# Rounds of outer products turned over, their bias moved into the relu, and every relu of the loop on ACT

## The reference

```python
x = e; xk = x; outs = []
for i in range(3):
    z = jnp.einsum('bfe,bge->bfge', x, xk).reshape(B_, F_ * F_, E_)   # products of fields f and g
    z = jnp.swapaxes(z, 1, 2)
    z = jnp.einsum('bcl,oc->bol', z, Ws[i]) + bs[i][None, :, None]    # sum over c, the 256 numbers e, for each pair l
    z = jnp.sum(jax.nn.relu(z), axis=-1)
    outs.append(z)                                                    # 16 numbers a sample
    xk = jnp.broadcast_to(z[:, :, None], (B_, F_, E_))
h = jnp.concatenate([outs..., dense_ctx], axis=1)                     # 48 + 16 features
h = jnp.maximum(h @ W_top1 + b_top1, 0.0)
h = jnp.maximum(h @ W_top2 + b_top2, 0.0)
y = h @ W_top3
```

## Time and profile before

| | |
|---|---|
| median of 3 runs | 565.79 us |
| the profiled execution | 566.43 us |
| its span (first to last instruction) | 564.6 us |
| PE busy / DVE / ACT / POOL | 536.8 / 524.9 / 404.4 / 452.8 us |
| granted clock of TensorE | 1.0 of full speed |
| a group in the steady part of the loop | 32.9 us |

### The profile page before, as it was taken

The page is one execution under the profiler, slowest core; times in us unless marked ns, Lnnn a source line. Parts: engine busy times, 40 slices in busy tenths (PEclk is TensorE's granted clock), DMA queues, the critical chain, the costliest instruction groups (busy, mean ns, idle before and its releaser), DMA issues.

```text
span 564.6 us, 19182 instructions
## 1 busy us (share of the span) xinstructions
PE 536.8 (95%) x8160; PEld 331.5 (59%) x8160; DVE 524.9 (93%) x234; ACT 404.4 (72%) x1217; POOL 452.8 (80%) x548
## 2 busy tenths in 40 slices
PE   2776899999999999999999999999999999999997
PEld 1433455666656566665656666565666656566566
DVE  5899899999999999999999999999999999999752
ACT  3575685877878687787868688786877778687743
POOL 6899999897988989798897979889897988988100
PEclk9999999999999999999999999999999999999999
DMA  3622323232232322223232222323232222322000
GB/s 91 172 73 70 91 67 92 63 72 81 67 80 65 96 58 75 79 66 81 64 96 58 69 85 67 79 65 96 58 76 76 64 82 68 91 63 63 17 2 2
DMA packets 27974, 40.67 MB, mean 72 GB/s; under 512 B 16880, under 2 KB 17264, under 8 KB 27888
## 3 DMA queue, kind: packets, MB, share of 16 engines
q0 software_dynamic: 12288, 33.57, 21.0%
q1 hardware_dynamic: 15600, 5.87, 4.7%
HBM read 38.77 MB, written 0.66 MB: 70 GB/s over the span
## 4 chain that ended last, share of the span: by engine, by line
PE 84%; POOL 7%; issue 4%; DVE 3%; DMA 1%; ACT 1%; POOLq 0%; DVEq 0%
PE sum_ps L701 39%; PE turn_ps L681 11%; PE outer_ps L776 9%; PE outer_ps L799 6%; PE sum_ps L716 4%; PE outer_ps L788 4%; POOL emb L291 4%; PE outer_ps L760 3%; DVE prods L237 2%; PE outer_ps L824 2%; POOL prods L304 1%; POOL prods L237 1%; PE outer_ps L808 1%; PE sum_ps L724 1%; PE sum_ps L710 1%
## 5 line engine op out<-in xcount | busy, mean ns | idle before, releaser
L237 DVE TENSOR_TENSOR prods<-turn_ps,emb_t 128x3360 f32<-128x3360 f32 (+2 forms) x126 | 452.7, 3608 | 11.9 <-ACT emb_t L518 10.1
L291 POOL DMA_INDIRECT emb<-tables,rows_sb x256 | 252.1, 985 | 44.1 <-issue 36.2
L701 PE MATMUL sum_ps<-prods,w_sb 128*32 128x272 f32 x4096 | 263.0, 398 | 1.1 <-POOL prods L237 1.0
L701 PEld LDWEIGHTS sum_ps<-prods,w_sb 128*32 128x32 f32 x4096 | 121.0, 110 | 96.0 <-issue 14.3
L545 ACT ACTIVATE relu<-sum_ps,bias_twice 128x120 f32<-128x120 f32 x256 | 91.6, 368 | 92.9 <-PE sum_ps L701 92.3
L304 POOL TENSOR_TENSOR prods<-emb_t 128x256 f32<-128x256 f32 x128 | 95.4, 746 | 32.1 <-ACT emb_t L518 30.0
L517 ACT COPY emb_t<-turn_ps 128x512 f32<-128x512 f32 (+1 forms) x126 | 75.7, 601 | 39.1 <-PE turn_ps L681 19.9
L681 PE MATMUL turn_ps<-ident_sb,emb 128*128 128x128 f32 x502 | 83.2, 288 | 9.2 <-issue 3.7
L237 POOL TENSOR_TENSOR prods<-emb_t 128x224 f32<-128x224 f32 (+1 forms) x128 | 83.9, 655 | 2.1
L556 ACT ACTIVATE relu_k<-outer_ps 128x2048 f32<-128x2048 f32 x44 | 83.8, 1904 | 2.2 <-PE outer_ps L776 2.2
L535 ACT ACTIVATE prods<-emb_t 128x512 f32<-128x512 f32 x128 | 83.7, 654 | 0.2
(11 more groups left out here) (99 smaller groups left out, 288.7 us busy)
## 6 DMA issues: line engine op xcount, KB each, us to landing
emb<-tables,rows_sb POOLq DMA_INDIRECT x256
z_wide<-z_spread SPq DMA_DIRECT2D x15, 256.0 KB
z_spread<-z_cat SPq DMA_DIRECT2D x60, 2.0 KB
w_sb<-w_top SPq DMA_DIRECT2D x1, 512.0 KB
z_spread<-z_wide SPq DMA_DIRECT2D x2, 256.0 KB
w_sb<-w_top SPq DMA_DIRECT2D x1, 256.0 KB
ids_sb<-ids_t SPq DMA_DIRECT2D x1, 129.0 KB, 2.2
z_cat<-dense_b SPq DMA_DIRECT2D x1, 128.0 KB
```

Source lines behind the costliest of these rows:

```text
L237: eng.tensor_tensor(out, every, shifted, ALU.mult).then_inc(done, 1)
L291: nc.gpsimd.indirect_dma_start(out=emb[:, k % EMB_RING, t * E:(t + 1) * E], out_offset=None, in_=tables, in_offset=bass.IndirectOffsetOnAx ...
L701: last = nc.tensor.matmul(sum_ps[s * 2 * F:(s + 1) * 2 * F, k % 2, 0:SUM_COLS], w_sb[:, c, odd, :], x[:, c, 2 * s + odd, :, :], start=c == ...
```

## The change

The two operands of a round's products trade places. `proj_b` becomes the stationary operand (its columns are picked with a step of two, since k is now innermost) and `z_wide` the moving one, 512 columns wide. So (f, o) come out on the partitions, 8 f x 16 o to a round, and (g, sample) along the columns. The output o is then a matter of the partition, and the bias is an operand `bias_k[:, k]` of the relu, one number per partition. The bias matmuls are gone, and so are their preparation on DVE, two loads in SP's queue, and the memset of the ones tile on POOL. A round is four fp32 matmuls of 512 columns in place of four bf16 ones of 512 and eight fp32 ones of 256.

All four relus of a group's rounds are on ACT; `relu_add` is gone. The fold of layer 2 therefore takes both rounds, as that of layer 1 does. After the fold, `reduce_fields` sums into a small tile `z_sum` and then transposes it into `z_cat`, two DVE instructions in place of one, with a wait between them. The columns of `z_cat` change places (dense features first). The wait for `z_wide` of layer 0 (`z_wide_in`) moves from the round into the last quarter of the same slot's `sum_pairs`.

```diff
@@ relu on ACT
-                nc.scalar.activation(relu_k[:, k, q, :, :, :].rearrange("p j h n -> p (j h n)"),
-                                     outer_ps[:].rearrange("p j n -> p (j n)"), ACT.Relu).then_inc(outer_relu, 1)
+                nc.scalar.activation(relu_k[:, k, q, :, :].rearrange("p j n -> p (j n)"), outer_ps[:].rearrange("p j n -> p (j n)"),
+                                     ACT.Relu, bias=bias_k[:, k:k + 1]).then_inc(outer_relu, 1)
@@ ACT's loop
-                if slot - 1 in ROUND_AT and (ROUND_AT[slot - 1][0], ROUND_AT[slot - 1][2]) != (1, 1):
+                if slot - 1 in ROUND_AT:
                     relu_round(*ROUND_AT[slot - 1])
@@ DVE
-            def relu_add(g):
...
-                nc.vector.scalar_tensor_tensor(out=second, in0=outer_ps[:].rearrange("p j n -> p (j n)"), scalar=0.0,
-                                               in1=first, op0=ALU.max, op1=ALU.add).then_inc(outer_relu, 1)
-            def reduce_fields(k, g):
+            def reduce_fields(k, g, src):
                 dve.wait_ge(fold_done[k], g + 1)
-                nc.vector.tensor_reduce(z_cat[:, g, (k + 1) * F:(k + 2) * F],
-                                        outer_ps[:, FOLD_BANK[k], 0:P].rearrange("p (f o) -> p o f", o=F),
-                                        AX.X, ALU.add).then_inc(z_ready[k], 1)
+                nc.vector.tensor_reduce(z_sum[:, k, :], src.rearrange("p (r a) -> p r a", r=R), AX.X, ALU.add).then_inc(z_summed[k], 1)
+                dve.wait_ge(z_summed[k], g + 1)
+                if k == 1:
+                    dve.wait_ge(z_ready[0], g + 1)
+                nc.vector.transpose(z_cat[:, g, Z_AT[k + 1]:Z_AT[k + 1] + R], z_sum[:, k, :]).then_inc(z_ready[k], 1)
@@ PE, sum_pairs
+                                if (c, odd, s) == (1, 1, 1) and (g := group_at(k, ROUNDS[0])) is not None:
+                                    pe.wait_ge(z_wide_in, 16 * (g + 1))
@@ PE, a round
-                b = bias_wide[:, k, :].rearrange("p (h n) -> p h n", h=1).broadcast_to([P, HALF_G, F * F])
-                for j in range(J):
-                    if q == 0 and j == 0:
-                        pe.wait_ge(proj_ready if k == 0 else z_ready[0], g + 1)
...
-                    if q == 0 and j == 3 and k == 0:
-                        pe.wait_ge(z_wide_in, 16 * (g + 1))
-                    if q == 0 and j == 3 and k == 1:
-                        pe.wait_ge(z_wide_ready[1], g + 1)
-                    nc.tensor.matmul(outer_ps[:, j, :], ones_sb[j * R:(j + 1) * R, :], b[j * R:(j + 1) * R, :, :],
-                                     start=True, stop=False)
-                products_of_round(k, g, q, [outer_ps[:, j, :] for j in range(J)])
+                for j in ((2, 3, 0, 1), (0, 1, 2, 3))[k]:
+                    if q == 0 and j == 2 and k == 0:
+                        pe.wait_ge(proj_ready, g + 1)
+                    if q == 0 and j == 0 and k == 1:
+                        pe.wait_ge(z_wide_ready[1], g + 1)
...
+                    last = outer_product(k, g, q, j, outer_ps[:, j, :])
+                last.then_inc(outer_done, 1)
+            def outer_product(k, g, q, j, out):
+                y = proj_b[j * R:(j + 1) * R, g % PT_RING, :].rearrange("p (n k) -> p k n", k=2)
+                return nc.tensor.matmul(out, y[:, k, q * HALF_F * F:(q + 1) * HALF_F * F],
+                                        z_wide[j * R:(j + 1) * R, k, :, :].rearrange("p q n -> p (q n)"), start=True, stop=True)
@@ PE, fold
-                first = k * HALF_G
-                for q in range(first, G4):
-                    for half in range(2):
-                        for j in range(J):
...
+                for q in range(TURNS):
+                    last = add_round(k, q, outer_ps[:, FOLD_BANK[k], 0:P], q == 0, q == TURNS - 1)
+            def add_round(k, q, out, first, final):
+                for n in range(G4):
+                    for j in range(J):
+                        last = nc.tensor.matmul(out[j * R:(j + 1) * R, :], fold_sb[:], relu_k[:, k, q, j, n * P:(n + 1) * P],
+                                                start=first and n == 0, stop=final and n == G4 - 1)
```

More of the change, by code:

```diff
@@ L340, in _ @@
                 half_shift(slot + 1)
+                if (g := group_at(slot, Z_BUILD)) is not None:
+                    z_spread(g)
                 gather(slot + 1 + LEAD, 1)
@@ L709, in turn_features @@
                 for half in range(2):
[L710 removed]
+                    last = nc.tensor.matmul(out[half * CAT:(half + 1) * CAT, :], z_cat[:, g, 0:CAT], ident_sb[:], start=True, stop=True)
                 last.then_inc(z_t_done, 1)
```

149 lines of the change are left out of this document (42 added, 107 removed).

## The result

The changed kernel takes 577.67 us, the median of four runs (576.91 to 581.25), against 565.76 us for the kernel before beside it. The ratio of the means is 1.0225, with a 95% interval of 1.0189 to 1.0261, a fifth run of 578.50 us included: slower by 2.2%, while the two medians are 2.1% apart. The forecast was 576.0 us with a range of 570 to 580. The profiled execution is the slowest of the four, 581.25 us with a span of 579.4; it is 14.8 us above the span of before, while the medians are 11.9 apart. Beyond the other traces of rounds turned over it has a late start, which is told further down.

The account below looks back on a forecast made before the run. PE was taken to bound the loop, with ACT holding stretch D. Twelve groups at +0.83 gave +9.9; start +0.4, last group +0.4, end -0.4: +10.3 on 566.43, 576.7, as a median 576.0 us, range 570 to 580.

Parts of the forecast that it names:

- the fold: Layer 2's fold on PE takes both rounds, 64 records instead of 32: +0.875 us a group, on PE's path.
- The round at 1.06 to 1.07: A round on PE drops its bias matmuls but loads its first weights bare: 1.06-1.07 us instead of 1.20, saving about 0.12.
- Two rounds of layer 2 save 0.24: On PE, layer 2's two shorter rounds were to take 0.24 us off each steady group.
- POOL's tie "as today": Layer 2's round waits for POOL's spreading of z at its first matmul, not its fourth: 0.01 us later at most.
- Stretch D, +0.22: From layer 1's first-round pair sum to its fold, held by ACT: 7.65 us plus 0.22 for bias in two relus.
- The relu on ACT at nothing: The 1.9 us relu that DVE gives up to ACT in slot 18 costs nothing; ACT's free time soaks it up.
- The moved wait, at something in the first group alone: Wait for z_wide's DMA, about half a microsecond earlier, in the pair sums: +0.8 us in the first group, where it bit once.
- The start, +0.4, bounds -0.5 to +1.0: First group: moved wait +0.8, fold +0.3, a vanished wait for DVE -0.6; taken as +0.4 us as a whole.
- The last group and the end, 0 together: Last group +0.4 us, with no fold behind its D; end section -0.4, from four shorter rounds less one reduction's 0.1.
- B: Rival: PE alone decides, ACT's chain has slack, all four round savings count; +0.33 us a group, 570 us; chance 0.16.
- C: Rival: DVE is the true pacer, so losing its relu speeds the loop; 556 us; chance 0.06 together with a weaker form, 564.
- E: Rival: strided weights or long reductions push groups over +1.2 us, PE waiting for DVE at slot 23; 580-584 us; chance 0.08.

## Why the prediction was right, and where not

The step that carries the result is the fold. It was put at +0.875 a group; two runs give 0.87 (halved in the changed kernel) and 0.83 (alone in the kernel before, which takes in DVE's small gain). The period was to be 33.75 and is 33.73, and 33.90 on the other chip. There the time, 579.86, is at the upper end of the range.

*The round at 1.06 to 1.07.* 1.08. The loads stand bare once the bias is gone: they start at 317.31, with the round, where before they started at 309.73, 0.21 us ahead of the first product. The strided weights cost nothing that shows. By the weight-load rule of the Trainium skill's page "TensorE: Matmul & The Clock Gate", section "LDWEIGHTS (loading the stationary operand)", which gives 107 ns for these loads, the saving was to be 0.12, and it is. The record of such a load is longer than that, 190 ns for 128 columns and 110 for the 32 of the folds. The difference is 0.83 ns a column, which is the page's rate.

*Two rounds of layer 2 save 0.24.* From the fold of layer 1 to that of layer 2 it is 329.77 - 309.33 = 20.44 us, and was 322.40 - 301.72 = 20.68. That is 0.24. What I did not see is why they could be saved at all: in the kernel before, the same saving alone is eaten by POOL and DVE. It shows in the changed kernel since DVE had been rid of its relu and POOL's `z_spread` had been moved ahead. The working had POOL's tie "as today"; in fact POOL has 1.8 us to spare. No run undoes that move alone, so how the saving divides between the two is not shown.

*Stretch D, +0.22.* D grew by 7.84 - 7.65 = 0.19. PE waits 0.45 where "some 0.5" was said, and both halves were taken away apart: the bias (-0.18 of period) and ACT's other work (-0.46). Here the profile before had decided it, by two times that met in one place, 334.60 and 334.65.

*The relu on ACT at nothing.* Right for the period (33.72 with it on DVE) and wrong for the whole. ACT's free time does soak it up before D: it had waits of 2.08 and 1.47 us, and in the changed group one of 2.03 is left ahead of D. But ACT's copy of z, which starts the chain of transfers to `z_wide`, is queued behind it. I followed DVE's copies there and not this one.

*The moved wait, at something in the first group alone.* This is the step that failed, and the total came out right all the same. The timeline of SP's queue in the two kernels, from the issue of the first small transfer to that of the large one; first the kernel before, then the changed one:

```profile
319.50 2.01 SPq L270 DMA_DIRECT2D z_spread<-z_cat  x4
323.50 0.34 SPq L274 DMA_DIRECT2D z_wide<-z_spread  x1
```

```profile
293.62 1.88 SPq L258 DMA_DIRECT2D z_spread<-z_cat  x4
296.75 0.34 SPq L262 DMA_DIRECT2D z_wide<-z_spread  x1
...
327.37 2.66 SPq L258 DMA_DIRECT2D z_spread<-z_cat  x4
331.69 0.34 SPq L262 DMA_DIRECT2D z_wide<-z_spread  x1
...
429.73 1.74 SPq L258 DMA_DIRECT2D z_spread<-z_cat  x4
435.00 0.34 SPq L262 DMA_DIRECT2D z_wide<-z_spread  x1
```

Before, these 4.0 us are the longest of the steady groups, and the others lie at 3.3 to 3.6. After, it is 3.1 in one group and 4.3 in the next, and in the latter the pair sums at 333.11 wait for it. The five groups with a late transfer are the five with 4.3 to 5.3; the others have 3.1 to 3.6. With the wait put back, four neighbouring groups still have 4.4 to 5.4, and next to nothing is lost. So the transfers are long in either case, and it is the place of the wait that turns them into a loss. I had seen that this wait bit once, and took one bite in 15 for the rule. Why some transfers take longer than any of the kernel before is not shown.

*The start, +0.4, bounds -0.5 to +1.0.* The first fold begins at 73.90 in the profiled execution (71.79 before), but at 70.4 to 72.1 in the traces of the other kernels with the rounds turned, and at 70.51 in the other trace of this same kernel. So the 73.90 belong to this execution and not to the moved wait. The row that answers to the earlier trace rows shows the wait at its new place:

```profile
64.54 0.66 PE L651 MATMUL sum_ps<-prods,w_sb 128*32 128x272 f32 x6 [2.08 <-DMA z_wide<-z_spread]
```

*The last group and the end, 0 together.* They cost 0.7: from the last fold of layer 1 to the end of the span it is 579.4 - 513.76 = 65.6 us, and was 564.6 - 499.70 = 64.9. The fold is in it with 0.86, so the rest saved 0.2 and not the 0.9 of the working; the full fold alone in the kernel before gives 65.8. What ate the savings there is open.

The profiled execution adds up. Its first steady fold comes 2.5 us later (106.66 against 104.17); 12 periods cost 0.80 each, 9.6; the late transfers add 2.3, less 0.4 of the kernel before's own; the end 0.7. Together 14.8, the difference of the spans. In the run with the wait put back the same places give -0.4, +9.1 and +0.8, 9.5 in all: nearly the predicted +10.3. The forecast of the median is 1.7 us low. It had nothing for the late transfers, about 2 us in this execution, and nothing for the end, 0.7. That it is as near as it is comes in part by luck: with the wait put back the start gave -0.4 and not +0.4, and most other traces have a first fold as early.

Of the rivals, B (570 us) had its PE and lacked ACT. C, DVE as the pacer, was excluded by the fold on its own costing the full 0.83 in the kernel before. But its core was closer than I had it: the run without the bias shows that DVE stands 0.15 us behind PE. E did not come in the first trace, where PE is not idle for DVE's products in the steady groups. On the other chip it came in small: PE waits for them at the very transposes that the working gave 0.25 us to spare, because DVE was 0.7 us late.

## What to carry to other kernels

When two engines meet in a row of the timeline, the one that a change shortens gains nothing there, and the cure is often order, not work: putting 0.7 us of ACT's work behind the relu (306.55 to 307.23 in the first trace) gave 0.46 us a group. A merging addition on a busy but not bounding engine may be what keeps work off the bounding one: ask what the sum costs on the engine that inherits it. And a wait for a transfer is best placed behind what releases other engines, since there the slack of later meetings can still absorb it.

## What the runs showed of the hardware

The time of the large transfer through DRAM isn't a constant: in the same kernel 3.1 to 5.3 us pass between the first small write's issue and the read's in steady groups, 5.3 in one and 3.4 in the next. The stream transpose of 128 x 32 takes 0.21 us, against 0.71 for 128 x 512. Wide or narrow moving operands, and weights with a column step of two, make no difference to a round of the same number of columns, 1.07 and 1.08 us. And the same kernel had a period of 33.73 us in one trace and 33.90 on another chip, where the same 64 matmuls released DVE 2.70 us after their start and not 1.99.
